# All eight experts' weights split during the attention units, and unit 0's first scores one preparation step later

## The reference

```python
xn = layernorm(x)
q = xn @ Wq.T;  kv = xn @ Wkv_down.T;  k = kv @ Wk_up.T;  v = kv @ Wv_up.T   # 8 heads of 32, latent 64
attn = softmax(q k^T * 32**-0.5) @ v, then @ Wo.T          # over the 256 tokens of a sequence
idx = mod(floor(xn @ wr + br), 8)                          # one expert per token
ffn = relu(xn @ W1[idx] + b1[idx]) @ W2[idx] + b2[idx]     # 128 -> 512 -> 128, 8 experts
out = x + attn + ffn
```

## Time and profile before

| | us |
|---|---|
| median of 3 runs (range) | 505.51 (501.59 to 506.85) |
| the profiled execution | 505.35 |
| its span, first to last instruction | 503.5 |
| busy: PE, DVE, POOL, ACT | 456.6, 414.5, 376.5, 346.0 |
| preparation, to the first exponential of unit 0 | 0 to 51.8 |
| units 0 to 15 | 51.8 to about 220 |
| experts' stage | about 220 to 336 |
| units 16 to 31 | 336 to 503.5 |

### The profile page before, as it was taken

One profiled execution on the slowest core, in us unless ns is written; L12 is line 12 of the kernel. 1 busy time (PEld: TensorE's weight loads), 2 busy tenths in 40 slices (PEclk: granted clock), 3 DMA queues, 4 the chain that ended last, 5 costly groups with the idle time before them and its releaser, 6 DMA issues.

```text
span 503.5 us, 15093 instructions
## 1 busy us (share of the span) xinstructions
PE 456.6 (91%) x4992; PEld 319.7 (63%) x4992; DVE 414.5 (82%) x883; ACT 346.0 (69%) x861; POOL 376.5 (75%) x399
## 2 busy tenths in 40 slices
PE   1868879999999999979999999998999989999967
PEld 1446445665656646658999999964665656656634
DVE  6998988778899899848888888875899898898865
ACT  3686457766777878847777777755766777687654
POOL 4755388888888888717777777757898888988952
PEclk9985899999999999989999999998999999999999
DMA  7994923565573896797878888726474566656322
GB/s 227 331 219 121 270 72 104 125 125 129 145 215 106 204 260 193 224 239 218 262 254 258 262 262 273 227 76 121 89 149 114 132 133 133 129 131 137 84 73 65
DMA packets 82826, 86.74 MB, mean 172 GB/s; under 512 B 10608, under 2 KB 66384, under 8 KB 82768
## 3 DMA queue, kind: packets, MB, share of 16 engines
q1 hardware_dynamic: 78672, 77.60, 57.2%
q0 software_dynamic: 4096, 8.40, 6.7%
HBM read 38.61 MB, written 22.04 MB: 120 GB/s over the span
## 4 chain that ended last, share of the span: by engine, by line
PE 43%; issue 16%; DVE 14%; POOL 13%; DMA 5%; ACT 4%; SPq 3%; POOLq 1%; ACTq 0%; DVEq 0%
POOL padd L592 12%; PE psum L1286 9%; PE psum L1251 8%; PE psum L1270 7%; DVE negm L990 6%; PE psum L1328 4%; PE psum L1301 4%; DMA stk<-mT 4%; SPq L326 3%; PE psum L1199 3%; PE psum L1200 2%; PE psum L1201 2%; DVE split L914 2%; ACT prob L724 2%; PE psum L1220 1%
## 5 line engine op out<-in xcount | busy, mean ns | idle before, releaser
L724 ACT ACTIVATE prob<-psum 128x512 f32<-128x512 f32 x256 | 150.2, 593 | 97.8 <-PE psum L1270 70.4
L990 DVE TENSOR_REDUCE negm<-psum 128x2 f16<-128x512 f32 x256 | 170.6, 682 | 43.3 <-PE psum L1251 36.2
L644 POOL TENSOR_TENSOR padd<-prob 128x512 f32<-128x512 f32 x104 | 126.6, 1218 | 34.6 <-ACT prob L724 26.3
L1251 PE MATMUL psum<-stk 96*128 96x256 f16 x512 | 101.6, 281 | 12.0 <-DVE negm L990 9.4
L592 POOL TENSOR_TENSOR padd<-xTl,padd 128x512 f16<-128x512 f32 x71 | 82.2, 1157 | 36.4 <-DVE padd L1100 36.4
L1270 PE MATMUL psum<-stk 97*128 97x256 f16 x512 | 97.8, 274 | 9.7 <-DMA stk<-mT 4.7
L794 ACT ACTIVATE xTl<-psum,xn_all 128x128 f32<-128x128 f32 x284 | 81.1, 369 | 27.5 <-POOL padd L592 20.7
L610 POOL DMA_INDIRECT xsort<-xn_all,pos x64 | 67.5, 1055 | 14.1 <-issue 13.5
L624 POOL DMA_INDIRECT xn_all<-ysort,pos x64 | 65.4, 1021 | 15.2 <-issue 7.7
L1251 PEld LDWEIGHTS psum<-stk 96*128 96x128 f16 x512 | 41.7, 98 | 54.6 <-DVE negm L990 25.8
L1286 PE MATMUL psum<-prob,vt 128*32 128x256 f32 x1024 | 70.5, 391 | 0.9 <-ACT prob L724 0.8
(11 more groups left out here) (166 smaller groups left out, 882.4 us busy)
## 6 DMA issues: line engine op xcount, KB each, us to landing
stk<-split SPq DMA_DIRECT2D x192, 128.0 KB
xn_all<-wsplit SPq DMA_DIRECT2D x71, 258.0 KB, 4.4
xsort<-oT SPq DMA_DIRECT2D x9, 512.0 KB, 4.9
xTh<-xsort SPq DMA_DIRECT2D x18, 256.0 KB, 4.0
ysort<-xTh SPq DMA_DIRECT2D x18, 256.0 KB, 4.2
out<-acc SPq DMA_DIRECT2D x15, 256.0 KB
acc<-x SPq DMA_DIRECT2D x3, 1024.0 KB, 8.4
xn_all<-W SPq DMA_DIRECT2D x12, 256.0 KB
```

The source lines that it names most:

```text
L644: nc.gpsimd.tensor_tensor(padd[:, bb, hs], prob[:, bb, hs, 0, :], prob[:, bb, hs, 1, :], ALU.add).then_inc(pool_add, 1)
L724: nc.scalar.activation(prob[:, bb, h, :, :].rearrange("p a c -> p (a c)"), bank[st_bank(u, n)], ACT.Exp, scale=SCALE).then_inc(act_exp, 1)
L990: V.tensor_reduce(negm[:, k % 2, col:col + 2], bank[n % 2].rearrange("p (a c) -> p a c", a=2), AX.X, ALU.max, negate=True).then_inc(dve_ma ...
L1251: ins = mm(bank[n % 2][:, qc * T:(qc + 1) * T], stk[0:96, s, 1, h, t0 + qc * P:t0 + (qc + 1) * P], stk[0:96, s, 0, h, t0:t0 + T], start=Tr ...
```

## The change

The preparation loses both experts' loads, splits and stores, and ScalarE's wait for those stores. All eight experts go through the late path: 0 in unit 6, 1 in unit 8, 2 to 7 in units 9 to 14; the first two are loaded in unit 5. Expert 7's store is thereby issued in unit 15, and `first_weights` and the last two second-layer loads go to unit 15 behind it. The two parts of the tiles' list move from units 6 and 8 to units 4 and 5. Units 11 to 13 scatter five chunks instead of four, so unit 14 has one left. In the preparation unit 0's scores begin in step 7, with heads 0 and 1 together, and the row maxima in step 8, with two of them; unit 2's key projection in step 6 waits for one low part less.

```diff
@@ constants
-    WSTEP = (8, 10)
-    EARLY = len(WSTEP)
-    LATE_AT = {2: 7, 3: 9, 4: 10, 5: 11, 6: 12, 7: 13}
+    LATE_AT = {0: 6, 1: 8, 2: 9, 3: 10, 4: 11, 5: 12, 6: 13, 7: 14}
@@ SyncE
-            def load_weights(e):
-                sp.dma_start(wstage[e][:, 0:F], W1[e]).then_inc(sp_w[e], 16)
-                sp.dma_start(wstage[e][:, F:2 * F].rearrange("p (c d) -> p c d", c=FC),
-                             W2[e].rearrange("(c p) d -> p c d", p=P)).then_inc(sp_w[e], 16)
...
-            def store_weights(e):
-                sp.wait_ge(dve_wl, e + 1)
-                sp.dma_start(wsplit[e, :, 0:F], wout_f[e][:, 0:F]).then_inc(sp_ws[e], 16)
-                sp.dma_start(wsplit[e, :, W1E // 2:], wout_f[e][:, F:2 * F]).then_inc(sp_ws[e], 16)
...
             def load_late(e):
                 i = e % 2
-                if e >= EARLY + 2:
-                    sp.wait_ge(dve_lw, e - EARLY - 1)
+                if e >= 2:
+                    sp.wait_ge(dve_lw, e - 1)
...
             def early_weights(u):
-                if u == 6:
+                if u == 5:
                     for par in range(2):
                         sp.wait_ge(pool_scat[par], 128)
-                        load_late(EARLY + par)
+                        load_late(par)
...
-                if u == 14:
+                if u == 15:
                     first_weights()
-                if u == 15:
                     load_w2(E - 2)
                     load_w2(E - 1)
...
             ex = []
-            for e in range(EARLY):
-                load_weights(e)
             sp.wait_ge(dve_set, 1)
...
             for j in range(4):
-                if j == 3:
-                    for e in range(EARLY):
-                        store_weights(e)
                 sp.dma_start(stk[96:97, j, 0, :, :], ones16[4 * j:4 * j + 4, :]).then_inc(sp_ones, 16)
@@ GpSimd, scatters_at
-                return (1, 3, 5, 7) if 11 <= u < 14 else (0, 1, 3, 5, 7)
+                return (0, 1, 3, 5, 7)
@@ ScalarE
-            def expert_weights(e):
-                act.wait_ge(sp_w[e], 32)
-                nc.scalar.activation(wblk[e][:, :, 0, :], wstage[e].rearrange("p (b n) -> p b n", b=8),
-                                     ACT.Copy, scale=WS).then_inc(act_w, 1)
...
             def late_weights(e):
                 i = e % 2
-                act.wait_ge(sp_lw[i], 32 * ((e - EARLY) // 2 + 1))
-                if e >= EARLY + 2:
-                    act.wait_ge(sp_ls[i], 32 * ((e - EARLY) // 2))
+                act.wait_ge(sp_lw[i], 32 * (e // 2 + 1))
+                if e >= 2:
+                    act.wait_ge(sp_ls[i], 32 * (e // 2))
                 else:
                     act.wait_ge(pool_scat[i], 128 * 2)
...
-                if s in WSTEP:
-                    expert_weights(WSTEP.index(s))
-            for e in range(EARLY):
-                act.wait_ge(sp_ws[e], 32)
             body(0, True, False)
@@ VectorE
-            def weights_low(e):
-                dve.wait_ge(act_w, e + 1)
-                V.scalar_tensor_tensor(wblk[e][:, :, 1, :], wstage[e].rearrange("p (b n) -> p b n", b=8), WS,
-                                       wblk[e][:, :, 0, :], ALU.mult, ALU.subtract).then_inc(dve_wl, 1)
...
-                            if u in (6, 8) and n == 6:
-                                tile_experts(u // 2 - 3)
+                            if u in (4, 5) and n == 6:
+                                tile_experts(u - 4)
...
-                if 7 <= s < 15:
+                if s == 8:
+                    row_max(0, 0, 0)
+                if 8 <= s < 15:
                     row_max(0, s - 7, 0)
...
-                if s in WSTEP:
-                    weights_low(WSTEP.index(s))
@@ TensorE, the preparation's steps
                 if s == 6:
-                    pe.wait_ge(dve_kl, 2)
+                    pe.wait_ge(dve_kl, 1)
                     proj_k(2, 1, 2)
...
                 token_keys(s - 3)
-                if s == 6:
+                if s == 7:
                     pe.wait_ge(dve_kl, 2)
                     pe.wait_ge(dve_ql, 2)
-                if 6 <= s < 14:
+                    scores(0, 0, 0, 0)
+                if 7 <= s < 14:
                     scores(0, s - 6, 0, 0)
```

More of the change, by code:

```diff
@@ L104, in attention_moe_block @@
         padd_f = padd[:, :, :, :].rearrange("p a b c -> p (a b c)")
-        wraw = stk_f[:, 12288:16384].bitcast(F32)
-        wstage = [wraw[:, 0:1024], wraw[:, 1024:2048]]
-        wout_f = [prob_f[:, 0:1024], prob_f[:, 2560:3584]]
-        wblk = [w.bitcast(F16).rearrange("p (b s n) -> p b s n", b=8, s=2) for w in wout_f]
         wq_f, wkup_f, wvup_f = prob_f[:, 1024:1280], prob_f[0:R, 1280:1536], prob_f[0:R, 1536:1792]
@@ L164, in attention_moe_block @@
         sp_zero = sem("sp_zero")
-        sp_w = [sem(f"sp_w{i}") for i in range(2)]
-        sp_ws = [sem(f"sp_ws{i}") for i in range(2)]
         sp_wf = sem("sp_wf")
@@ L307, in store_late @@
                 i = e % 2
-                sp.wait_ge(dve_lw, e - EARLY + 1)
+                sp.wait_ge(dve_lw, e + 1)
                 sp.dma_start(wsplit[e, :, 0:F], lout[i][:, 0:F]).then_inc(sp_ls[i], 16)
                 sp.dma_start(wsplit[e, :, W1E // 2:], lout[i][:, F:2 * F]).then_inc(sp_ls[i], 16)
-            def store_weights(e):
-                sp.wait_ge(dve_wl, e + 1)
-                sp.dma_start(wsplit[e, :, 0:F], wout_f[e][:, 0:F]).then_inc(sp_ws[e], 16)
-                sp.dma_start(wsplit[e, :, W1E // 2:], wout_f[e][:, F:2 * F]).then_inc(sp_ws[e], 16)
             def load_max(w, k):
@@ L348, in load_w2 @@
                 sp.wait_ge(pool_scat[g % 2], 128 * (g // 2 + 1))
-                if e >= EARLY:
-                    sp.wait_ge(sp_ls[e % 2], 32 * ((e - EARLY) // 2 + 1))
+                sp.wait_ge(sp_ls[e % 2], 32 * (e // 2 + 1))
                 sp.dma_start(wf32[:, e * F:(e + 1) * F], wsplit[e, :, W1E // 2:]).then_inc(sp_wf, 16)
             def early_weights(u):
-                if u == 6:
+                if u == 5:
                     for par in range(2):
                         sp.wait_ge(pool_scat[par], 128)
-                        load_late(EARLY + par)
+                        load_late(par)
                 if u - 1 in LATE:
@@ L414, in first_weights @@
                 for i in range(2):
-                    sp.wait_ge(sp_ls[i], 32 * ((E - EARLY) // 2))
+                    sp.wait_ge(sp_ls[i], 32 * (E // 2))
                 for t in range(NB):
@@ L1040, in late_low @@
                 i = e % 2
-                dve.wait_ge(act_lw, e - EARLY + 1)
+                dve.wait_ge(act_lw, e + 1)
                 V.scalar_tensor_tensor(lblk[i][:, :, 1, :], lraw[i].rearrange("p (b n) -> p b n", b=8), WS,
```

2 lines of the change are left out of this document (removed).

## The result

The changed kernel takes 507.96 us (median of 13 runs, 504.51 to 512.15) against 505.63 for the kernel before (13 runs in the same session, 501.59 to 506.85): a ratio of 1.0048, 95% interval 1.0024 to 1.0071. (All ratios here leave out executions more than 1.5% above the fastest of their kernel.) The forecast was 507.4. The profiled execution took 508.35 us, its span is 506.5.

A forecast was written before the change was run, and what follows sets the result against it. TensorE, busy 91% of the span, was taken as the bound. Preparation -1.4, units +1.65 and seam +1.6 sum to +1.85 on 505.35: 507.2 us, as a median 507.4, range 502 to 512.

The forecast's parts named there:

- (a) to (c): Preparation: ScalarE still waits for the stack, step 8's row maxima delay step 9, then two-step loops set the pace: -1.4 us.
- Rival B: Preparation gives back all the chain shows, -5.4, as TensorE's clock stays up; seam without stall: 500.1 us, chance 0.08.
- the hole of step 6: Preparation: TensorE's 2.03 us wait for the stack before unit 0's first scores, predicted to go from step 6.
- +1.65: Units: sum of what the attention units pay for the experts and list parts moved into or among them, in us.
- Pairs 4-5, 10-11 and 12-13: Units: tile-count parts cost 4-5 +0.5 us; 10-11 stays; one more scatter each costs 12-13 +0.2.
- units 6 and 7 lose the 2.38 us and move the expert from the odd to the even unit: 0: Units 6 and 7: VectorE's list part leaves, the expert changes unit; no net cost, bounds -0.4 and +0.5 us.
- Unit 14's +0.95: Unit 14 gets an expert; ScalarE has no slack there, VectorE's part fits: +0.95 us, bounds +0.5 and +1.1.
- up to 0.9 us more: Units: sharing GpSimd's SBUF interface, each moved expert costs VectorE this much above the preparation, already held in the windows.
- Rival C: Units pay more: VectorE in unit 4 runs late, GpSimd's scatters hold sums; +3.8 instead of +1.65, 509.5 us, chance 0.09.
- 1.1 us later than 229.20: Seam: expert 7's late store delays the loads, so the experts' stage's first output comes at 230.3.
- I had priced that as added: Seam: TensorE's hole of some 3.5 us before the first output brings a low-clock stretch, +0.5 us, bounds 0 and 1.7.
- Rival A: Seam decides and is slower: slow second-layer loads put the first output at about 234.8; 511.9 us, chance 0.13.

The follow-up runs named there:

- experiment 2: Changed kernel with the scores' part undone (unit 0's scores from step 6), all eight experts still in the units: 501.85 us, ratio 1.0026 to the kernel before.
- experiment 3: Changed kernel with unit 15's expert store, first-layer and last second-layer loads issued ahead of unit 18's stack: 497.36 us, ratio 0.9947 to the kernel before.
- experiment 5: The changed kernel itself run again, unaltered, on another chip: 506.61 us, ratio 1.0035 to the kernel before.
- experiment 6: Changed kernel with unit 0's scores back in step 6 and unit 15's expert store and loads ahead of unit 18's stack: 503.18 us, ratio 0.9982 to kernel before.
- experiment 9: Same program as experiment 6 (scores from step 6, unit 15's expert transfers ahead of the stack), on another chip: 504.69 us, ratio 1.0001 to the kernel before.
- experiment 1: Kernel before with only the scores' part (scores from step 7, row maxima from step 8, one low part less awaited): 499.42 us, ratio 0.9989.
- kernel 7: Kernel before with the seam's order alone (token groups, then experts' loads in unit 15, then unit 18's stack); experts 0 and 1 stay: 504.06 us, ratio 0.9975.
- experiment 10: Experiment 9 with GpSimd's scatters at n = 0, 1, 2, 3, 7 instead of 0, 1, 3, 5, 7: median 510.05 us; ratio 0.9927 from two of twelve runs.
- experiment 12: Kernel 7 with GpSimd's scatters at n = 0, 1, 2, 3, 7 (1, 2, 3, 7 in units 11 to 13): 514.75 us, ratio 1.0198 to kernel before.
- experiment 4: Changed kernel with ScalarE's part of each expert's split cut to an eighth, weights not the real ones: 501.13 us, ratio 1.0015 to the kernel before.
- experiment 8: Changed kernel with VectorE's part of each expert's split cut to an eighth, weights not the real ones: 514.49 us, ratio 1.0192 to the kernel before.
- experiment 11: Experiment 9 with VectorE's low part in two halves, at n = 6 and n = 7: 504.40 us, ratio 0.9987 to the kernel before.

## Why the prediction was right, step by step

The total was 0.6 us off, and that is luck: three errors offset each other (preparation 0.5 too good, units 0.8 too cheap, seam 0.7 too dear, by this profile), and so did the two pieces that nobody forecast, +1.43 and -1.14. The direction was right; that the total was close doesn't show that its parts were. One profile alone is a poor ruler here, so I also use the profiles of the experiments as repeats of the parts that they share.

| part | forecast | this profile | mean over the profiles with and without the part |
|---|---|---|---|
| preparation (copies) | -1.4 | -0.9 | 33.59 (3) for 34.39 (3): -0.8 |
| pair 4-5 | +0.5 | +0.3 | 20.22 (6) for 19.79 (3): +0.4 |
| pair 6-7 | 0 | +0.5 | 21.44 (6) for 20.26 (3): +1.2 |
| pair 8-9 | 0 | -0.3 | 20.61 for 21.04: -0.4 |
| pair 10-11 | 0 | +0.1 | 21.26 for 21.30: 0 |
| pair 12-13 | +0.2 | +0.9 | 21.34 for 21.09: +0.25 |
| unit 14 | +0.95 | +0.9 | 10.65 for 9.37: +1.3 |
| unit 15 and experts' stage | +1.6 | +0.9 | 128.05 (3) for 127.37 (2): +0.7 |

With the change: the profiled kernel and experiments 2, 3, 5, 6 and 9; without: the kernel before and experiments 1 and 7. The preparation's three with the change are the profiled kernel and 3 and 5. The stage's groups leave out the kernels with the other order. The last column adds up to about +2.6 us, the medians differ by 2.3. The profiles come from several chips and single values scatter by some 0.5 us about these means (unit 6 reaches 11.55 in one), so a difference under that is not shown; in these profiles the values with and without the change lie apart in pair 6-7 (20.88 to 21.97 for 19.68 to 20.60), pair 8-9 (20.37 to 20.81 for 20.98 to 21.14) and unit 14 (10.38 to 10.91 for 9.14 to 9.51), and overlap in the others. Experiments 10 and 12 are left out, since the slots changed their units, and so are 4, 8 and 11.

- **Preparation, (a) to (c): the mechanism was right**, the size 0.5 us too good. Step 8's copy came at 32.32 (forecast 32.2), the third score waited 3.05 us (forecast some 3), step 9's copy at 35.91 (35.1 to 35.7), step 15's at 46.47 (46.2). Experiments 1 and 2 separate what the sum had mixed: -2.2 for the experts, +1.3 for the scores. Rival B needed the upper clock once the hole of step 6 was gone; the clock of that window is 0.50, and the -5.4 was not near. What the clock is worth there shows in experiment 10, whose preparation is that of 2, 6 and 9: its granted clock stayed at the upper level from 21.1 to 41.6 us, longer than in the others, and its copies took 30.71 us, for 32.28, 32.31 and 32.89.
- **Units: the term that was mis-sized.** +1.65 was forecast; the pairs with unit 14 paid +2.5 in this profile and +2.7 over all. Pairs 4-5, 10-11 and 12-13 came within the scatter of their forecasts over all (the +0.9 of 12-13 in this profile is mostly its own; GpSimd stood at 19.31 us there for 16.96). The mis-sized step is "units 6 and 7 lose the 2.38 us and move the expert from the odd to the even unit: 0". I let VectorE's saving cancel ScalarE's cost, though each engine has its own slack. Unit 14's +0.95 came as +0.9 in this profile and +1.3 over all. Unit 6 went from 9.38 to 10.29 us as a mean over the same profiles (medians 9.14 and 9.98), and without ScalarE's part it was 9.2 again (experiment 4). Unit 7, which lost its expert, gave nothing back (10.88 to 11.15), nor did VectorE's 3.0 us less in the pair (19.12 to 16.12), as it was not last there. The prediction added that an expert's low part costs up to 0.9 us more here than in the preparation; it was up to 1.3 us (2.51 for 1.23), and the last section says what lengthens it. The 9.90 us that unit 6 took in the profile before hid this: in experiments 1 and 7 it takes 9.14 and 9.10. Part of it came back in pair 8-9, -0.4, at the lower bound given. Rival C named the direction, units that pay more (here by 0.8 to 1.0 us), and the wrong place.
- **Unit 1's +1.43 us can't be charged to the change.** Its row shows the clock at 0.51 for 3.5 us; kernel 7, built on the kernel before, has the same (13.14 us), and experiments 3 and 9 do not (11.73 and 11.80). Over all profiles the long unit 1 stands in seven of ten with the change and in two of four without; whether the change makes it more frequent isn't known. Take it off, and the 4.11 us of this profile are 2.7.
- **Seam: the waits came, the late output did not.** The token group's wait of 2.64 us went and waits of 4.45 us for weights came, 2.06 of them at the first output; this is what was forecast, though in experiment 5 the same program waited there for 0.43 us only. Unit 15 began 3.19 us later than before (212.30 for 209.11); with that taken off, the store went out at 214.9 (forecast 215), the first load at 218.7 (219.4), and the first output came at 228.6 (230.3). The load was issued 3.8 us behind the store, not 4.4. So "1.1 us later than 229.20" was wrong in its sign: against unit 15 the first output came 0.6 us earlier than before (19.51 us for 20.09). The +0.9 us of this profile arose behind it, where the clock was low. I had priced that as added, and it had been paid before as well: ahead of the first output, now behind it. The window of the changed kernel:

```profile
231.90:235.40 3.50, 3.50 (x29) 3.16 (x29) 1.16 (x4) 0.74 (x3) 1.16 (x1) 0.53 0.71 251
```

  From the first output to unit 16 it took 109.21 us here, with that stretch behind the output, and 109.20 and 109.33 in experiments 4 and 3, which have it there too; it took 107.70 before, with the stretch ahead, and 107.58 to 108.31 in all eight profiles without a low clock behind the output. Experiment 5, the same program as this profile, is one of them (low from 227.1 to 230.5, output at 232.3): 127.29 us in all, 0.5 us under the kernel before. The mean of +0.7 is therefore within what one program does from run to run (127.29 to 128.72 with the change, 126.94 and 127.79 without), and the seam's cost isn't shown. Rival A, an output after 233.5, did not come, nor did rival B: step 15's copy was not before 45.

**What a better version is.** Experiment 3 beat the kernel before (0.9947, 0.9920 to 0.9974). With the preparation's scores also put back, 0.9982 and 1.0001 on two chips: no proof of more, though the copies are 0.7 to 1.3 us shorter. Why the shorter preparation doesn't show in the medians is open; the kernels' own runs spread over 4 to 9 us. What the record supports: the order at the seam gives back about the change's loss. Times fell by 4.5 us between 2 and 3 on one chip and by 3.4 us between 5 and 6 on another, and both pairs differ in the preparation's scores as well, in opposite directions; unit 15 and the experts' stage took 123.49 to 127.80 us in the five profiles of 3, 6, 9, 10 and 11 with this order, and 127.29 to 128.72 in the three of the changed kernel, 2 and 5 without it.

## What to carry to other kernels

Moving a piece of work out of a stage gains only down to the next wait: put each removed wait beside the one that is queued next on the same engine (here a row maximum in front of a transposition) before counting it. Where work on two engines moves in opposite directions in one unit, price each engine against its own slack, and don't let them cancel. When a producer moves later, look at what stands ahead of its store in the one DMA queue; putting it ahead of seven other DMAs went with a gain of the size of what the change had cost.

## What the hardware showed that I had not expected

GpSimd's additions and VectorE's low parts (two inputs in SBUF, 128 x 1024) hold each other up. In units 9, 11 and 13 this looks like an effect of the scatters, since a low part of 1.9 us or more nearly always has a scatter over its end. It is the addition. VectorE's timeline of the changed kernel, units 11 and 12:

```profile
177.49 2.51 DVE L1000 SCALAR_TENSOR_TENSOR xn_all<-xn_all 128x1024 f16<-128x1024 f32 x1
187.78 1.22 DVE L1000 SCALAR_TENSOR_TENSOR xn_all<-xn_all 128x1024 f16<-128x1024 f32 x1
```

GpSimd beside them:

```profile
177.63 1.29 POOL L617 TENSOR_TENSOR padd<-prob 128x512 f32<-128x512 f32 x1
179.08 1.78 POOL L583 DMA_INDIRECT xsort<-xn_all,pos  x1 [0.17 <-PE psum L1259]
...
187.33 0.99 POOL L583 DMA_INDIRECT xsort<-xn_all,pos  x1 [0.17 <-issue]
188.34 1.79 POOL L617 TENSOR_TENSOR padd<-prob 128x512 f32<-128x512 f32 x1
```

In unit 11 the addition keeps its 1.29 us, and the low part ends 1.1 us after it. In unit 12 the low part keeps its 1.22 us, and the addition, begun inside it, takes 1.79 and ends 1.1 us after it. All 88 low parts of full size in this study are one or the other: 46 take 1.57 to 2.98 us and end 1.08 to 1.10 us after an addition of 1.26 to 1.30 us; 42 take 1.21 to 1.26 us, and the addition begun inside them takes 1.37 to 2.01. A scatter isn't needed for it (unit 14 of experiment 4, 1.97 us) and does not do it: in unit 6 of experiment 10 one starts with the low part, at 124.15, and they take 0.98 and 1.26 us. A scatter that starts inside a long low part is itself held up, 1.78 us for 0.98, and ends 0.86 us after it. The Trainium skill ("GPSIMD Engine Reference", the table of its first part) says that GpSimd shares its SBUF interface with VectorE when VectorE has two SBUF inputs; these rows agree. Which of the two goes first isn't settled by who starts first in the profile: additions that begin up to 0.62 us after the low part went first in some units. So the engines do not meet at semaphores only, as the first section has it.

And the same program draws between two lengths of a unit: 11.8 us in unit 1 of experiment 9 and 13.3 us in 6, with a stretch of low clock in the long one (3.5 us at 0.51 in the changed kernel). Such draws are of the size of the whole effect under study.
